# Attention with fewer TensorE sums: additions by GpSimd and by accumulating DMAs, maxima over two PSUM banks

## The reference, cut to what matters

```python
qkv = (h @ Wqkv + bqkv).reshape(B, L, 3, H, HD)     # B 2, L 2048, H 16, HD 32, float32
q, k, v = jnp.moveaxis(qkv, 2, 0)
attn = jnp.einsum('blhd,bmhd->bhlm', q, k) * HD ** (-0.5)
attn = jax.nn.softmax(attn, axis=-1)
out = jnp.einsum('bhlm,bmhd->blhd', attn, v).reshape(B, L, D)
```

## Time and profile before

| | |
|---|---|
| median of the runs | 3694.41 us |
| profiled execution: span | 3696.8 us |
| PE busy | 3452.4 us, 93% of the span |
| DVE busy | 2266.1 us, 61% |
| POOL busy | 1775.8 us, 48% |
| ACT busy | 1552.4 us, 42% |
| 1445 to 1501 us (one half): PE, DVE, ACT, POOL busy | 54.88, 45.48, 34.37, 46.14 of 56 us |

### The profile page before, as it was taken

The page is one execution under the profiler, slowest core; times in us unless marked ns, Lnnn a source line. Parts: engine busy times, 40 slices in busy tenths (PEclk is TensorE's granted clock), DMA queues, the critical chain, the costliest instruction groups (busy, mean ns, idle before and its releaser), DMA issues. The chain is left out here.

```text
span 3696.8 us, 51173 instructions
## 1 busy us (share of the span) xinstructions
PE 3452.4 (93%) x17516; PEld 2197.3 (59%) x17516; DVE 2266.1 (61%) x3547; ACT 1552.4 (42%) x2751; POOL 1775.8 (48%) x527
## 2 busy tenths in 40 slices
PE   7899996997999999999999999999995779999999
PEld 6488885775544444444444444444434658888887
DVE  1378874444978788788788887887715932222222
ACT  0111114341166666666656666666662242222222
POOL 1033321001288788787887887877885500000000
PEclk9999998997699999999999999999997889999999
DMA  4122224446201222102222022200004641111100
GB/s 163 66 93 88 91 80 172 172 158 183 46 17 34 43 47 44 38 16 44 47 48 44 7 44 47 47 10 13 7 6 154 216 146 68 40 40 40 37 32 23
DMA packets 158137, 250.59 MB, mean 68 GB/s; under 512 B 46939, under 2 KB 68699, under 8 KB 151774
## 3 DMA queue, kind: packets, MB, share of 16 engines
q1 hardware_dynamic: 147166, 230.96, 21.1%
q10 hardware_dynamic: 10752, 16.79, 1.5%
HBM read 158.89 MB, written 88.08 MB: 67 GB/s over the span
## 5 line engine op out<-in xcount | busy, mean ns | idle before, releaser
L1147 DVE TENSOR_REDUCE att_mx<-att_pM 128x1 f32<-128x512 f32 x2048 | 1267.9, 680 | 336.2 <-PE att_pM L1213 334.0
L1104 ACT ACTIVATE att_prob<-att_pS 128x512 f32<-128x512 f32 x2048 | 1080.4, 601 | 772.8 <-PE att_pS L1261 765.2
L1083 POOL TENSOR_TENSOR att_acc<-att_acc,att_prob 128x2048 f32<-128x2048 f32 x288 | 1327.5, 4609 | 129.2 <-ACT att_prob L1104 104.1
L1213 PE MATMUL att_pM<-att_ks,att_qs 96*128 96x512 f32 x2048 | 855.1, 432 | 54.7 <-DVE att_mx L1147 33.6
L1261 PE MATMUL att_pS<-att_qs,att_ks 98*128 98x512 f32 x2048 | 868.8, 430 | 10.2 <-ACT att_prob L1104 8.0
L1261 PEld LDWEIGHTS att_pS<-att_qs,att_ks 98*128 98x128 f32 x2048 | 386.2, 190 | 555.1 <-ACT att_prob L1104 385.7
L1228 PE MATMUL att_pO<-att_prob,att_V 128*32 128x512 f32 x4096 | 548.7, 608 | 0.7 <-ACT att_prob L1104 0.7
L1213 PEld LDWEIGHTS att_pM<-att_ks,att_qs 96*128 96x128 f32 x2048 | 405.4, 198 | 200.5 <-DVE att_mx L1147 120.3
L1627 DVE TENSOR_TENSOR mlp_us<-mlp_tu,mlp_us 128x512 fp32r<-128x512 f32 x128 | 89.7, 700 | 536.0 <-ACT mlp_us L1600 536.0
L1670 PE MATMUL mlp_pu<-mlp_hs,mlp_W 128*128 128x512 f32 x1536 | 370.7, 391 | 18.9 <-DVE mlp_W L1619 18.9
L1689 PE MATMUL mlp_pa<-mlp_W,mlp_us 128*128 128x512 f32 x1536 | 368.8, 389 | 0.0
(11 more groups left out here) (181 smaller groups left out, 2984.7 us busy)
## 6 DMA issues: line engine op xcount, KB each, us to landing
qk_d<-qkv_qs SPq DMA_DIRECT2D x64, 512.0 KB, 2.7
att_qs<-qk_d SPq DMA_DIRECT2D x48, 512.0 KB, 7.4
att_ks<-qk_d SPq DMA_DIRECT2D x48, 512.0 KB, 13.8
gat_xT<-in_xT SPq DMA_DIRECT2D x32, 256.0 KB, 3.1
gat_xrow<-in_x SPq DMA_DIRECT2D x32, 256.0 KB, 2.8
x_d<-gat_x SPq DMA_DIRECT2D x32, 256.0 KB, 2.1
qkv_xr<-x_d SPq DMA_DIRECT2D x8, 1024.0 KB, 5.8
v_d<-qkv_vs SPq DMA_DIRECT2D x32, 256.0 KB, 2.0
```

The costliest lines, as they stand in the source:

```text
L1083: nc.gpsimd.tensor_tensor(acc[half][:], old[:], new[:], ALU.add).then_inc(added, 1)
L1104: nc.scalar.activation(prob[step % PR][:, c, :], pS[n % 3][:], ACT.Exp, scale=SCALE).then_inc(exp_done, 1)
L1147: nc.vector.tensor_reduce(mx[:, n // 4, n % 4:n % 4 + 1], bank(g, n)[:], AX.X, ALU.max).then_inc(m_read, 1)
L1213: nc.tensor.matmul(bank(g, n)[:], qs[k][0:KD, h, t * P:(t + 1) * P], ks[k][0:KD, h, mc * 512:(mc + 1) * 512], start=True, stop=True).then_ ...
```

## The change

- Six steps of a half (SENT: 2, 4, ..., 12) are summed by DMA: SP copies the first prob tile into a new buffer `gathered` (`send_first`, 1 MB SBUF to SBUF), GpSimd issues five accumulating DMAs that add the others to it (`send`), each waiting for the one before. GpSimd adds the other ten steps into `acc` (nine additions). TensorE sums only `gathered` and `acc`, two blocks behind the values block in step 4 of the next half (`finish`), into a slot of the `pS` ring; `pZ` is gone.
- `pM` is two buffers of two banks. Two maxima matmuls (c = 0, 1 and c = 2, 3) fill one, and one reduce 128x1024 reads it.
- ScalarE copies the sums to `rec`. Rows are equal within 32 partitions, so SP packs four rows to 128x16 (`reciprocals`), VectorE takes one reciprocal (`invert`, step 6), SP writes it to DRAM and reads it back, spread to 32 partitions each. GpSimd multiplies by `oc` (`scale`), SP stores (`store`).
- `prob` has eight buffers instead of four, q and k three instead of four, loaded two groups ahead. The hardware loops are unrolled.

```diff
-        NM = 2 * MT * 4
-        MS = NM // ST
+        NQ = 2 * MT * 2
-        U = 4
-        PR = 4
-        ADDED = [0, 1, 2, 4, 5, 6, 8, 9, 11, 12, 13]
+        U = 3
+        PR = 8
+        SENT = [2, 4, 6, 8, 10, 12]
+        ADDED = [t for t in range(MT) if t not in SENT]
         NA = len(ADDED) - 1
-        FINISH = 2
-        INVERT = 4
+        FINISH = 4
+        INVERT = 6
+        SCALED = 5
...
-        pM = [m.ps(f"pM{i}") for i in range(3)]
-        pO, pZ = m.ps("pO"), m.ps("pZ")
+        pM = [m.ps(f"pM{i}", [P, 2, 512]) for i in range(2)]
+        pO = m.ps("pO")
...
+        def wait_bank(pe, at):
+            if at >= 2:
+                pe.wait_ge(m_read, at - 1)
...
+            def send_first(n):
+                step = n % 2 * MT + SENT[0]
+                sp.wait_ge(exp_done, exps(n // 2, step))
+                if n >= 1:
+                    sp.wait_ge(exp_done, turns_of[n - 1] + 1)
+                sp.dma_start(gathered[:], prob[step % PR][:]).then_inc(first_sent, 16)
+            def reciprocals(n):
+                sp.wait_ge(exp_done, turns_of[n] + 1)
+                for c in range(4):
+                    row = rec[c * HD:c * HD + 1, :].rearrange("a (i x) -> a i x", x=16)
+                    sp.dma_start(packed[c * HD:(c + 1) * HD, :], row).then_inc(z_packed, 16)
+                sp.wait_ge(inverted, n + 1)
+                sp.dma_start(io["z_d"][n % 2].rearrange("c (i x) -> (c i) x", x=16), packed[:]).then_inc(z_kept, 16)
+                sp.wait_ge(z_kept, 16 * (n + 1))
+                for c in range(4):
+                    sp.dma_start(rec[c * HD:(c + 1) * HD, :], io["z_d"][n % 2, c:c + 1, :].to_broadcast([HD, 512])).then_inc(z_spread, 16)
...
+            for g in range(NG):                       # SP
+                if g >= 1:
+                    sp.wait_ge(step_done, g * ST)
+                    if g + 2 < NG:
+                        load(g + 2)
+                    if g + 1 < NG:
+                        load_v(g + 1)
+                    send_first(2 * g)
+                    reciprocals(2 * g - 1)
+                    store(2 * g - 1)
+                else:
+                    send_first(0)
+                send_first(2 * g + 1)
+                reciprocals(2 * g)
+                store(2 * g)
+                if g + 1 < NG:
+                    rows(g + 1)
...
+            def send(n, j):                           # GpSimd
+                step = n % 2 * MT + SENT[j]
+                pool.wait_ge(exp_done, exps(n // 2, step))
+                if j == 1:
+                    pool.wait_ge(first_sent, (n + 1) * 16)
+                else:
+                    pool.wait_ge(sent, (n * (len(SENT) - 1) + j - 1) * 16)
+                nc.gpsimd.dma_start(gathered[:], prob[step % PR][:], accum_op=ALU.add).then_inc(sent, 16)
...
                         nc.gpsimd.tensor_tensor(acc[half][:], old[:], new[:], ALU.add).then_inc(added, 1)
+                        if ADDED[i] - 1 in SENT[1:]:
+                            send(n, SENT.index(ADDED[i] - 1))
+                        if i == SCALED and n >= 1:
+                            pool.wait_ge(added, n * NA + i)
+                            scale(n - 1)
...
-                nc.vector.tensor_reduce(mx[:, n // 4, n % 4:n % 4 + 1], bank(g, n)[:], AX.X, ALU.max).then_inc(m_read, 1)
+                nc.vector.tensor_reduce(mx[:, q // 2, q % 2:q % 2 + 1], bank(at)[:], AX.XY, ALU.max).then_inc(m_read, 1)
...
+            def finish(n):                            # TensorE
+                at = turns_of[n]
+                pe.wait_ge(exp_done, at - 2)
+                pe.wait_ge(sent, (n + 1) * (len(SENT) - 1) * 16)
+                sums(pS[at % 3], gathered, True, False)
                 pe.wait_ge(added, (n + 1) * NA)
+                sums(pS[at % 3], acc[n % 2], False, True).then_inc(s_done, 1)
...
+                pair = m_pair(g, step, c // 2)        # in scores, behind the score c
+                if pair:
+                    maxima(*pair, c % 2)
```

More of the change, by code:

```diff
@@ L997, in bank @@
[L997 to L1014, removed]
@@ L1016, in half_before, with fill @@
-        def half_before(g, step):
-            return 2 * g + step // MT - 1
+            return (g + ahead, (step + LEAD) % ST * 2 + half) if g + ahead < NG else None
+        place = {}
+        def fill(what):
+            place[what] = len(place)
+        for q in range(NQ):
+            fill((0, q))
+        for q in range(EARLY):
+            fill((1, q))
+        fill("turned 0")
+        for q in range(EARLY, LEAD * 2):
+            fill((1, q))
+        for g in range(NG):
+            for step in range(ST):
+                if step == ST - LEAD + 1 and g + 1 < NG:
+                    fill(f"turned {g + 1}")
+                for half in range(2):
+                    if m_pair(g, step, half):
+                        fill(m_pair(g, step, half))
@@ new lines, in attention_phase, with score_turn, exps @@
+        turns_of = {}
+        def score_turn(what):
+            turns_of[what] = len(turns_of)
+        for g in range(NG):
+            for step in range(ST):
+                for c in range(4):
+                    score_turn((g, step, c))
+                    if c == 2 and step % MT == FINISH and (g or step >= MT):
+                        score_turn(2 * g + step // MT - 1)
+        score_turn(2 * NG - 1)
+        def exps(g, step):
+            return turns_of[g, step, 3] + 1
+        def turn(g):
+            return place[f"turned {g}"]
@@ new lines, in _ @@
+            load(0)
+            load(1)
+            load_v(0)
+            load_v(1)
+            load(2)
+            rows(0)
+            for g in range(NG):
+                if g >= 1:
+                    sp.wait_ge(step_done, g * ST)
+                    if g + 2 < NG:
[12 more added lines that the diff above has]
+                    rows(g + 1)
@@ L1060, in _ @@
+            reciprocals(2 * NG - 1)
+            store(2 * NG - 1)
+            for x in o_stored:
+                sp.wait_ge(x, 16 * 4 * NG)
         @block.gpsimd
@@ L1103, in body @@
[L1103 to L1117, removed]
-                    act.wait_ge(o_ready, n)
-                nc.scalar.activation(oc[:], pO[:], ACT.Identity).then_inc(o_copied, 1)
[L1121 to L1126, removed]
@@ L1292, in _ @@
-            behind(NG - 1, U - 1, ST - 1)
-            finish(NG, 0)
+                    for c in range(4):
+                        scores(g, step, c)
+                        if c == 2 and (g or step):
+                            behind(*divmod(g * ST + step - 1, ST))
+                            if step % MT == FINISH and (g or step >= MT):
+                                finish(2 * g + step // MT - 1)
+            behind(NG - 1, ST - 1)
+            finish(2 * NG - 1)
 def proj_phase(nc, io, keep):
```

324 lines of the change are left out of this document (156 added, 168 removed).

## The result

Median 3794.14 us (4 runs, 3789.2 to 3796.63) against 3699.17 for the kernel before, whose median a fourth run (3707.06) had moved up from 3694.41: ratio 1.0251, 95% interval 1.0233 to 1.0269. The forecast was 3737, +43 us; it came +95. The sign was right and the range held the time, but the size forecast was less than half of what came.

The account below looks back on a forecast made before the run. TensorE was taken to bound the attention, 56.5 us a half. Sums -3.73, long VectorE instructions -1.52 and bank wait +6.4 give +1.15, x 29.6 = +34; with -5, +10 and +4, +43: 3737 us, range 3630 to 3890.

Parts of the forecast that it names:

- The step (+6.4 a half): Maxima matmuls in the loop: TensorE waits for a pair of banks, +0.40 us a step, 16 steps, +6.4 us a half.
- the three terms: Bank wait: 0.43 from matmul start to reduce start, 1.21 for the reduce, 0.05 from its end to the next matmul.
- the follower's delay: Values block behind a held maxima matmul: follows after 0.43 us where 0.33 is usual, 0.10 more.
- Sums and `output`: Per half: fewer sums blocks on TensorE, -3.73 us; VectorE's long `output` and four reciprocals no longer delay it, -1.52 us.
- The DMA's duration T: Accumulating DMA, issue to landing: taken as 7 us between bounds 5.4 and 11.6, hidden; decides from 8.4.
- The sign that I named for T above 8.4: In the trace: GpSimd's additions waiting for a DMA, or exponentials waiting for a landing, would show T above 8.4 us.
- "I count 0" for the queue behind the loads: SP's first copy and packed-sums DMAs behind 3.5 MB of loads in even halves: VectorE's wait in step 6 counted 0.
- The given bound of 42: Other bound for SP's queue behind the loads: 3 us in 14 groups, +42 us.
- The maxima before the loop, -5: Before the loop: 76 pairs of maxima, each 0.07 us shorter with two-bank reduces, -5 us.
- The ends, +14: Last two halves, bound by GpSimd, +10 us; tail with three DMA hops and slower multiply for four reciprocals, +4.
- The rival "no wait at the bank", 3570: Maxima banks in the loop: no wait, GpSimd at 52 sets the half, 3570 us; smaller wait, faster, chance 0.17.
- 24 + 4T = 52: GpSimd's time per half: five additions and an issue, 24 us, plus four landings of T = 7 us.

## Why the prediction was right in sign and wrong in size

- *The step (+6.4 a half).* Right: 3.48, and the three terms, summed to 1.69, came to 1.72, with the follower's delay as the rows gave it. Copies with and without the wait confirm it as a cost: 182 us.
- *Sums and `output`.* Right: 1.72, and no long wait in step 8.
- *The DMA's duration T.* 7.3 against 7, but this was luck: I picked 7 between bounds of 5.4 and 11.6 and no row had an accumulating DMA. The sign that I named for T above 8.4, GpSimd waiting for a DMA, was no sign either: with T at 7.3 it waits 124 us for landings in the loop, and they are hidden.
- *"I count 0" for the queue behind the loads.* Wrong, +23 us, the largest miss. I let the loads land within 17 to 20 us, a time from the kernel before, issued the first copy at 17, had VectorE want the packed sums from about 25, and took the near tie for free. In the changed kernel the loads share the engines with accumulating DMAs: they land after 22 to 24 us, the first copy takes 9.2 to 10.4 instead of 4.7, and VectorE wants the sums at about 24.4 and gets them 1.8 to 3.1 later. Moving the loads, moving the reciprocal, or copying instead of adding each takes the wait in step 6 away. The given bound of 42 held it.
- *The maxima before the loop, -5.* Wrong in sign, +6. TensorE runs there at the lower clock (granted 0.50 over this stretch in both kernels). Timeline of all engines after:

```profile
905.69 2.36 DVE L1218 TENSOR_REDUCE att_mx<-att_pM 128x1 f32<-128x1024 f32 x2 [0.18 <-PE att_pM L1272]
...
906.97 2.36 PE L1272 MATMUL att_pM<-att_ks,att_qs 96*128 96x512 f32 x4 [0.19 <-DVE att_mx L1218]
```

  Four matmuls take 2.36 us and stand 0.19 for the reduce, and VectorE stands 0.18 for them. With two buffers, refilling one (about 1.2 us at this clock, and the handovers) takes a little longer than the 1.18 us of one reduce, so each engine waits for the other. I used only VectorE's rate. Three single banks gave 91.6 us again, and the shorter reduce 77.0. That the clock is what makes the refill too long is read from these rows, no run changes it.
- *The ends, +14.* Measured +27: the last two halves up to the last values block +6 (forecast +10), what stands behind it +21 (forecast +4). The timeline of all engines:

```profile
2858.45 0.20 PEld L1289 LDWEIGHTS att_pO<-att_prob,att_V 128*32 128x32 f32 x8 [1.19 <-ACT att_prob L1203]
...
2861.31 0.88 POOL L1134 DMA_DIRECT2D att_gathered<-att_prob  x1 [0.91 <-DMA att_gathered<-att_prob]
...
2868.78 0.88 POOL L1134 DMA_DIRECT2D att_gathered<-att_prob  x1 [2.07 <-DMA att_gathered<-att_prob]
...
2875.84 1.93 PE L1295 MATMUL att_pS<-att_gathered,att_ones 128*32 128x512 f32 x8 [15.46 <-DMA att_gathered<-att_prob]
2878.89 0.20 PEld L1295 LDWEIGHTS att_pS<-att_acc,att_ones 128*32 128x32 f32 x8 [2.85 <-POOL att_acc L1154]
...
2885.05 0.25 DVE L1237 RECIPROCAL att_packed<-att_packed 128x16 f32<-128x16 f32 x1 [52.45 <-DMA att_packed<-att_rec]
...
2890.52 1.26 POOL L1124 TENSOR_TENSOR att_o<-att_oc,att_rec 128x512 f32<-128x512 f32 x1 [11.68 <-DMA att_rec<-z_d]
...
2896.24 0.41 SPq L1392 DMA_DIRECT2D prj_stage<-in_Wproj  x1
```

  I priced the last two halves and the tail apart, each as if the other were on time. But GpSimd's chain is behind when TensorE's last values block (2858.45) starts: two more DMAs go out at 2861 and 2869, TensorE waits 15.46 us for the fifth and 2.85 more for GpSimd's last additions, and only then do the small hops begin. From the last values block to the last sums block it is 20.4 us (5.8 before), from there to the projection's first DMA 17.4 (11.0 before). So the hops and what stands beside them cost 6 more than before where I had 4, and the 15 us ahead of them were in no term. Copies in place of additions, with the order unchanged, bring the whole stretch from 156.6 to 132.4.
- *The rest:* 4 us are scatter ahead of the attention.
- *The rival "no wait at the bank", 3570.* Wrong as priced. I gave GpSimd's limit as 24 + 4T = 52 and left out that the chain closes: the fifth landing releases the closing sums and the exponentials of step 4, and behind them come those that the next second DMA needs. 4 x 7.7 + 7.3 + 13.6 = 52 is the same figure, but with the fifth at 17 it is 61 in every other half. With the pair filled ahead, the fifth landings are 51 to 57 us apart into opening halves, as this sum says, but 64 to 66 into the halves before a group with loads, and with the loads cut they are 53 to 58 apart in both. So the shape of the loop is shown, and 3 to 4 us of its length are not accounted for.

The mechanism of the forecast was right for the step, and the terms that failed are three covers that were called sufficient, or left out, by a few microseconds: the queue behind the loads (0, measured 23), the maxima before the loop (-5, measured +6), and the ends (14, measured 27). Together with the 4 us of scatter, 23 + 11 + 13 + 4 are 51 of the 52 us missed.

## What to carry to other kernels

A buffer pair that is filled across a long instruction block is held through that block. Count the time from its last write to the next request, not the load of the engine that reads it. When one bound is removed, price the next as a closed loop over all engines and DMAs that it passes, with the slowest neighbour on each: here removing one limit gained 7 us instead of 182, since the other lay right behind it. Count also who holds the buffers of a ring: here a late DMA held back not only its own sum but the exponentials that reuse its source. A near tie between a queue and its user is to be priced as a cost, and with the durations that the new traffic gives, not those of the old trace.

## What the runs showed of the hardware that was not expected

- A 1 MB accumulating DMA inside SBUF lands in 7.3 us (median) and, beside 3.5 MB of loads, in 15 to 18; a copy in 4.7, from either queue.
- The loads are slowed too: the same 3.5 MB were all landed 18 to 20 us after the first issue in the kernel before and with plain copies, and 22 to 24 with accumulating DMAs beside them.
- Waits of TensorE of 1.50 to 2.05 us in an otherwise full stretch were followed, in four of 13 opening halves, by 3.4 us at the lower clock (granted 0.62 over 4.5 us); one of 2.02 was not.
